# Node-ordered accumulator columns and one contiguous one-hot per edge tile in a two-layer graph network kernel

## The reference, cut to what matters

```python
h = relu(layernorm(x))                                    # stage 0
# two layers (layer 0, layer 1): norm = dis[src] * dis[dst], with a self loop for every node
h = h @ W
h = segment_sum(h[src] * norm[:, None], dst) + b
h = layernorm(tanh(h)) * g + be
x = x + h                                                 # after layer 1
h = relu(layernorm(x))                                    # layer 2 (edge features)
aggr = segment_sum(relu(h[src] + edge_attr), dst)
h = relu((h + aggr) @ W1 + b1) @ W2 + b2
out = x + relu(h)
```

## Time and profile before

| | |
|---|---|
| median of 3 runs | 2889.8 us (2885.09 to 2891.92) |
| the profiled execution | 2884.79 us, of which the span of the profile is 2883.0 us |
| mean granted TensorE clock | 0.899 |
| busy share of the span | PE 73%, PEld 65%, DVE 81%, ACT 70%, POOL 62% |
| DMA | 523.50 MB in all, mean 182 GB/s |

### The profile page before, as it was taken

How to read it: one execution, slowest core, us unless ns; L and a number is a source line. 1 busy time by engine, 2 the same in 40 slices (tenths; PEclk the granted TensorE clock), 3 DMA queues, 4 the chain that set the end, 5 groups by cost and what they waited for, 6 DMA issues and landing times.

```text
span 2883.0 us, 53972 instructions
## 1 busy us (share of the span) xinstructions
PE 2100.9 (73%) x15433; PEld 1879.5 (65%) x15433; DVE 2332.1 (81%) x8137; ACT 2016.7 (70%) x5708; POOL 1785.3 (62%) x2717
## 2 busy tenths in 40 slices
PE   0200028999999886577777777788289999999988
PEld 0100028888889876467667676677168888887877
DVE  4999848888889784499999799899868787777665
ACT  0039966888888594476666566667488999988766
POOL 4025667777777726787676765664377776765540
PEclk9999999999999887778888788878589999999879
DMA  0059957888888665245544455444356665655443
GB/s 14 1 216 383 370 199 239 280 278 279 277 286 283 206 241 168 78 148 157 157 150 145 144 158 157 125 150 138 123 143 179 181 177 171 173 166 158 142 116 104
DMA packets 262164, 523.50 MB, mean 182 GB/s; under 512 B 101225, under 2 KB 102260, under 8 KB 261864
## 3 DMA queue, kind: packets, MB, share of 16 engines
q1 hardware_dynamic: 217325, 451.15, 45.9%
q0 software_dynamic: 43680, 68.58, 11.0%
q10 hardware_dynamic: 859, 0.23, 0.0%
HBM read 324.98 MB, written 194.81 MB: 180 GB/s over the span
## 4 chain that ended last, share of the span: by engine, by line
PE 37%; DVE 28%; POOL 13%; ACT 12%; issue 6%; DMA 3%; SPq 1%; POOLq 0%; ACTq 0%; DVEq 0%
PE ps L1263 17%; POOL got_f_ L702 12%; DVE hot_ L938 7%; ACT rows_f_ L1079 6%; PE ps L1298 6%; PE ps L1308 5%; PE ps L1248 4%; DVE stat_b_ L873 4%; PE ps L1279 3%; DVE stat_a_ L873 3%; DMA got_f_<-table,src_of 3%; DVE hot_p_ L767 2%; DVE y_f_ L1002 2%; DVE low_f_ L912 2%; ACT rows_f_ L1116 1%
## 5 line engine op out<-in xcount | busy, mean ns | idle before, releaser
L702 POOL DMA_INDIRECT got_f_<-table,src_of x1365 | 1448.7, 1061 | 703.7 <-issue 369.4
L1263 PE MATMUL ps<-hot_,high_f_ 128*96 128x304 f32 (+46 forms) x3750 | 1020.7, 309 | 303.5 <-DVE hot_ L938 300.7
L1263 PE MATMUL ps<-hot_,low_f_ 128*96 128x304 f32 (+46 forms) x3750 | 991.2, 303 | 0.0
L1263 PEld LDWEIGHTS ps<-hot_,high_f_ 128*96 128x96 f32 (+1 forms) x3750 | 684.0, 182 | 381.7 <-issue 215.7
L938 DVE TENSOR_SCALAR hot_<-node_at,dst_of 128x368 fp32r<-128x368 f32 (+33 forms) x1875 | 837.7, 486 | 37.8 <-PE ps L1263 36.1
L1263 PEld LDWEIGHTS ps<-hot_,low_f_ 128*96 128x96 f32 (+1 forms) x3750 | 687.1, 183 | 32.4 <-issue 0.2
L1104 ACT ACTIVATE y_f_<-ps,ds 128x96 f32<-128x96 f32 x1568 | 386.5, 372 | 247.8 <-POOL rows_f_ L689 174.0
L1092 ACT COPY z_f_<-ps 97x1024 f32<-97x1024 f32 (+2 forms) x294 | 300.5, 1022 | 193.7 <-PE ps L1263 192.9
L1248 PE MATMUL ps<-ident_f,in_f_ 128*97 128x128 f32 (+1 forms) x1568 | 223.3, 290 | 265.5 <-DMA in_f_<-table 265.5
L873 DVE BATCH_NORM_STATS2 stat_a_<-y_f_ 128x6 f32<-128x96 f32 x1952 | 383.9, 242 | 2.9 <-ACT y_f_ L1104 2.9
L1248 PEld LDWEIGHTS ps<-ident_f,in_f_ 128*97 128x97 f32 (+1 forms) x1568 | 195.8, 179 | 265.8 <-DMA in_f_<-table 265.8
(11 more groups left out here) (117 smaller groups left out, 2816.3 us busy)
## 6 DMA issues: line engine op xcount, KB each, us to landing
x_f_<-in_x SPq DMA_DIRECT2D x146, 384.0 KB, 5.4
table<-rows_f_ SPq DMA_DIRECT2D x98, 396.0 KB
in_f_<-table SPq DMA_DIRECT2D x98, 396.0 KB
table<-rows_f_ SPq DMA_DIRECT2D x98, 392.0 KB
in_f_<-table SPq DMA_DIRECT2D x98, 392.0 KB
table<-rows_f_ SPq DMA_DIRECT2D x98, 388.0 KB
in_f_<-table SPq DMA_DIRECT2D x98, 388.0 KB
skip<-x_f_ SPq DMA_DIRECT2D x97, 384.0 KB, 3.5
```

The lines of the kernel that those rows point to most:

```text
L702: pool.indirect_dma_start(out=got_f[g][:, u * w:(u + 1) * w], out_offset=None, in_=table[:, :], in_offset=bass.IndirectOffsetOnAxis(ap=src ...
L1263: last = pe.matmul(acc[0:w, h, :].rearrange("m (s p) -> m s p", p=P)[:, :, p0:p0 + pw], part[:, u * wide_w:u * wide_w + w], hot_view(slot, ...
```

## The change

The partition order of a block is altered to two half blocks: slab group h (4 of the 8 slabs) holds nodes of half block h, and partition p holds nodes `512h + 4p` to `512h + 4p + 3` of it. With this, an accumulator column can be the node's own number in its block: column `c` of bank `h` is node `512h + c`. A transpose of slab s then writes columns `s % 4, s % 4 + 4, ...` (a step of four), one-hots are contiguous ranges of nodes, and `evict` reads the accumulator with a step of four and writes slabs in a row, so that `z_f` is as before. A one-hot is now made once for each tile (a tile whose band crosses into another block keeps its one-hot for the second block), and a pair has only the pieces (bank, first column, width, offset in the one-hot) that its band touches: two matmuls for each piece. Bands are rounded to 2 nodes and not to 16. Every plain transfer of a block moves 256 runs of half the length (1536 bytes for 96-wide rows) in place of 128. Transfers of the short last block to and from x and the output are two. The core of the diff:

```diff
-                lo = max(first, int(lo) // (2 * slabs) * 2 * slabs)
-                hi = min(stop, -(-math.ceil(hi) // (2 * slabs)) * 2 * slabs)
+                lo = max(first, int(lo) // 2 * 2)
+                hi = min(stop, -(-math.ceil(hi) // 2) * 2)
...
-                    for b in range(lo // block, -(-hi // block)):
-                        p0, p1 = (max(lo, b * block) - b * block) // slabs, (min(hi, (b + 1) * block) - b * block) // slabs
-                        use.append((place[b], q, u, b, p0, p1 - p0))
+                    cuts = [lo, hi] if hi - lo <= block else [lo, *range((lo // block + 1) * block, hi, block), hi]
+                    for lo, hi in zip(cuts, cuts[1:]):
+                        k = len(self.tiles)
+                        self.tiles.append((q, u, lo, hi))
+                        use += self.uses(place, block, k, lo, hi)
...
+    def uses(self, place, block, k, lo, hi):
+
+        found = []
+        for b in range(lo // block, -(-hi // block)):
+            pieces = []
+            for h in range(2):
+                bank = b * block + h * block // 2
+                c0, c1 = max(lo, bank), min(hi, bank + block // 2)
+                if c0 < c1:
+                    pieces.append((h, c0 - bank, c1 - c0, c0 - lo))
+            found.append((place[b], k, pieces))
+        return found
...
+        def move(eng, i, table, tile, done, load, whole=True):
+
+            lo = plan.at[i] * BLOCK
+            if whole or lo + BLOCK <= N:
+                far = table[ds(lo, BLOCK), :].rearrange("(h p q) d -> p h (q d)", h=2, q=S // 2)
+                near = tile[:, :, :].rearrange("p (h q) d -> p h (q d)", h=2)
+                eng.dma_start(near if load else far, far if load else near).then_inc(done, 16)
+                return
...
-                for m in plan.pairs_at[i]:
-                    q, u, b, p0, pw = plan.pairs[m]
-                    slot, turn = hot_slot(layer, m)
+                for k in plan.tiles_at[i]:
+                    q, u, lo, hi = plan.tiles[k]
+                    slot, turn = hot_slot(layer, k)
...
                     if turn >= HOTS:
-                        dve.wait_ge(pair_done, turn - HOTS + 1)
+                        b_layer, b_k = divmod(turn - HOTS, TILES)
+                        dve.wait_ge(pair_done, b_layer * PAIRS + plan.last_of[b_k] + 1)
                     c = plan.quads[q][1] + u
-                    dve.tensor_scalar(hot_view(slot, pw), node_at[:, :, 0:pw], float(b * BLOCK + p0 * S),
-                                      dst_of[:, c:c + 1], ALU.add, ALU.is_equal).then_inc(hot_ready_f, 1)
+                    dve.tensor_scalar(hot[slot][:, 0:hi - lo], node_at[:, 0:hi - lo], float(lo), dst_of[:, c:c + 1],
+                                      ALU.add, ALU.is_equal).then_inc(hot_ready_f, 1)
...
-                act.copy(z_f[i % 2][0:w, :].rearrange("p (h c) -> p h c", h=2), ps[done % 2][0:w, :, :]
-                         ).then_inc(evicted, 1)
+                act.copy(z_f[i % 2][0:w, :].rearrange("m (h q p) -> m h q p", h=2, q=S // 2),
+                         ps[done % 2][0:w, :, :].rearrange("m h (p q) -> m h q p", q=S // 2)).then_inc(evicted, 1)
...
-                    k = s % 4 * P
-                    last = pe.matmul(acc[0:w, s // 4, k:k + P], own[:, s, 0:w], ident_f[:, :], start=s % 4 == 0,
+                    to = acc[0:w, s // 4, :].rearrange("m (p q) -> m q p", q=S // 2)[:, s % 4, :]
+                    last = pe.matmul(to, own[:, s, 0:w], ident_f[:, :], start=s % 4 == 0,
...
-                    for h in range(2):
+                    for h, c0, n, a in pieces:
                         for part in (high_f[f], low_f[f]):
-                            last = pe.matmul(acc[0:w, h, :].rearrange("m (s p) -> m s p", p=P)[:, :, p0:p0 + pw],
-                                             part[:, u * wide_w:u * wide_w + w],
-                                             hot_view(slot, pw)[:, h * S // 2:(h + 1) * S // 2, :],
-                                             start=False, stop=m == plan.pairs_at[i][-1] and part is low_f[f],
-                                             skip_group_check=True)
+                            last = pe.matmul(acc[0:w, h, c0:c0 + n], part[:, u * wide_w:u * wide_w + w],
+                                             hot[slot][:, a:a + n], start=False,
+                                             stop=m == plan.pairs_at[i][-1] and part is low_f[f], skip_group_check=True)
```

More of the change, by code:

```diff
@@ L130, in __init__ @@
         self.first_place = [place[b] for b, _ in supers]
-        self.quads, self.pairs, self.pairs_at, use = [], [], [[] for _ in range(blocks)], []
+        self.quads, self.tiles, self.pairs, self.pairs_at, use = [], [], [], [[] for _ in range(blocks)], []
         for i in self.order:
@@ L140, in __init__ @@
                     lo, hi = self.bands[self.slot_of[i] + t + u]
[L141 to L146 removed]
+                    cuts = [lo, hi] if hi - lo <= block else [lo, *range((lo // block + 1) * block, hi, block), hi]
[3 more added lines that the diff above has]
+                        use += self.uses(place, block, k, lo, hi)
+        self.last_pair, self.first_use, self.last_use = [0] * len(self.quads), [blocks] * len(self.quads), [0] * len(self.quads)
+        self.first_of, self.last_of = {}, {}
+        self.tiles_at = [[] for _ in range(blocks)]
+        for m, (pos, k, pieces) in enumerate(sorted(use)):
+            q = self.tiles[k][0]
+            self.pairs.append((k, pieces))
             self.pairs_at[pos].append(m)
+            if k not in self.first_of:
+                self.first_of[k] = m
+                self.tiles_at[pos].append(k)
+            self.last_of[k] = m
             self.last_pair[q] = m
@@ L209, in gnn_kernel @@
     TILES_MAX = CHUNK
+    TILES = len(plan.tiles)
+    assert all(plan.last_of[k - HOTS] < plan.first_of[k] for k in range(HOTS, TILES))
+    assert max(hi - lo for _, _, lo, hi in plan.tiles) <= BLOCK
     assert GROUPS4 == 4 and SUPERS <= 128 and all(plan.pairs_at) and plan.at.index(BLOCKS - 1) >= X_RING + Y_RING
@@ L508, in table_written, with moved, hot_slot @@
                 eng.wait_ge(stored[j], stored_before(stage + 1, j))
[L510 to L515, removed]
+        def move(eng, i, table, tile, done, load, whole=True):
[5 more added lines that the diff above has]
+                return
+            for h in range(2):
+                rows_n = min(HB, N - lo - h * HB)
+                parts = rows_n // (S // 2)
+                far = table[ds(lo + h * HB, rows_n), :].rearrange("(p q) d -> p (q d)", q=S // 2)
+                near = tile[0:parts, h * (S // 2):(h + 1) * (S // 2), :].rearrange("p q d -> p (q d)")
+                eng.dma_start(near if load else far, far if load else near).then_inc(done, 16)
+        def moved(i, ring):
+            turns = range(i % ring, i + 1, ring)
+            return 16 * (len(turns) + (plan.at.index(BLOCKS - 1) in turns))
+        def hot_slot(layer, k):
+            n = layer * TILES + k
             return n % HOTS, n
@@ L643, in fast_sync @@
                     sp.wait_ge(out_done, k + 1)
-                    parts = parts_at(k)
-                    sp.dma_start(rows(out, plan.at[k], parts),
-                                 y_f[k % Y_RING][0:parts, :, :].rearrange("p s d -> p (s d)")
-                                 ).then_inc(out_stored[k % Y_RING], 16)
+                    move(sp, k, out, y_f[k % Y_RING], out_stored[k % Y_RING], False, whole=False)
             for j in range(Y_RING):
-                sp.wait_ge(out_stored[j], 16 * len(range(j, BLOCKS, Y_RING)))
+                sp.wait_ge(out_stored[j], moved(BLOCKS - 1 - (BLOCKS - 1 - j) % Y_RING, Y_RING))
         def prologue_pool(pool):
@@ L684, in add_x @@
                     k = i % X_RING
-                    pool.wait_ge(x_in_f[k], 16 * (len(range(k, BLOCKS, X_RING)) + i // X_RING + 1))
+                    last = k + (BLOCKS - 1 - k) // X_RING * X_RING
+                    pool.wait_ge(x_in_f[k], moved(last, X_RING) + 16 * (i // X_RING + 1))
                     if i % 4 == 0 and stored_before(2, i // 4):
@@ L976, in shift_x @@
                 k = i % X_RING
[L977 removed]
+                dve.wait_ge(x_in_f[k], moved(i, X_RING))
                 if i < X_RING:
@@ L1255, in gather_edges @@
                 for m in plan.pairs_at[i]:
-                    q, u, _, p0, pw = plan.pairs[m]
-                    slot, turn = hot_slot(layer, m)
+                    k, pieces = plan.pairs[m]
+                    q, u, _, _ = plan.tiles[k]
+                    slot, turn = hot_slot(layer, k)
                     f, quad_turn = high_slot(layer, q)
```

40 lines of the change are left out of this document (14 added, 26 removed).

## The result

The changed kernel takes 3047.9 us (median of 4 runs, 3038.5 to 3056.1) against 2887.5 us (2884.3 to 2891.9) for the kernel before on the same chip: ratio 1.0553 (95% interval 1.0518 to 1.0588). It is slower by 160 us; forecast were 51 us less. The profiled execution has a span of 3036.0 us at a mean granted clock of 0.875.

The account below looks back on a forecast made before the run. Bounds: ACT in stage 0, POOL's gathers in layer 0, DVE in most of layer 1, PE in layer 2. Gains of 2, 19 and 30 us sum to 51: 2889.8 - 51 = 2839 us, range 2808 to 2896.

Parts of the forecast that it names:

- One-hots: Making one-hots on DVE: 625 to 548 in a layer, 19 us less DVE work each; the ring's new wait costs nothing.
- that lead: Ring of one-hots: six tiles reach further than six pairs, and a block's first one-hot often exists already; wait costed at nothing.
- Its last sign of being wrong: Layer 1, where four engines wait on each other, moving by more than 30 us either way would show the prediction wrong.
- Layer 2: PE bounds it; 33 us less matmul work, less the block 87 rest and a little lost to ACT: 30 us gained.
- Block 87: Slow-clock block: PE's 27.65 us of matmuls would become 17, but DVE comes next at 22; 5.5 us taken.
- Layer 0: POOL's 455 gathers set the pace and do not change; only emptying the line after the last gather gains 2 us.
- Layer 1: DVE bounds most of it: 16 us from 19 us less one-hot work, plus 3 from block 87, 19 us gained.
- Rival B: PE pays for the step: transposes doubled, 1.04 us more a block, sum about +60, 2950 us; chance 0.09.
- Rival A: ACT pays for the step in the eviction, 7.6 us a block in layer 2: 2879 us, up to 2900; chance 0.14.
- Rival C: Layer 1: earlier one-hots and less PE work shorten the ring of waits by another 25 us, 2814 us; chance 0.13.
- Rival D: Layers 0 and 1 give savings back through less granted clock; smaller transfers cost stage 0 18 us: 2878 us; chance 0.09.
- The lead of 42 us: Stage 0: x is loaded 20 blocks ahead, 42 us, which covers up to 18 us of dearer half-length transfers.

Follow-up runs that it names:

- the ring in order: The renumbered kernel, but PE waits for the count that the old number by tile asked for, where higher: 2917.4 us, 1.0082 to the kernel before.
- the ring out of order: The changed kernel, numbers left as they are for the ring, but PE waits for the count at which its tile is made: 2840.6 us, 0.9833.
- the renumbered kernel: The changed kernel with tiles numbered in the order in which DVE makes their one-hots, ring and waits as they were: 2832.3 us, 0.9806.
- the longer ring: The changed kernel with one tile of 6144 one-hot columns given out by width in place of six buffers of 1024: 2921.8 us, 1.0129.
- a first experiment: The changed kernel with a one-hot for each (tile, block) pair again, 625 in a layer, same ring of six: 3229.8 us, 1.1212.

## Why the prediction was wrong, point by point

**The step that failed** is in "One-hots": "The ring of six now holds tiles, not pairs. The new wait, for a tile used in two blocks, can make DVE stand behind that tile's second block ... I cost it at nothing; the cover is that lead." It looked at one side, DVE's wait for a buffer, and took for granted that PE's wait for a one-hot still meant the one-hot that PE needs. Before, pairs were numbered in the order in which both engines went through them, and number and count were one; after, the number is the tile's, the order is still the block's, and they part where a band wider than a block is cut. The kernel's text shows it: `pe.wait_ge(hot_ready_f, turn + 1)` stayed as it was, while `turn` now came from the list of tiles, and DVE's loop over `tiles_at`. Printing the order of making against the numbers, an arithmetic like the one done for the matmuls, would have found 56 of 548 out of place. What it costs (85 us with the ring in order, 216 with it out of order) no row of before could have told; that it isn't nothing, the prediction's own sentence could have told: moments and row work stand between the one-hots of a block and those of the next. Its last sign of being wrong, layer 1 moving by more than 30 us, came true with 100. As the cover of the ring's wait, the lead held: alone, the ring out of order costs 8 us and a ring of four 13.

**The rest of the sum held**, in total, and that in part by luck: the renumbered kernel is what the prediction took the change to be, and has 2832 us, 55 less than before, where 2839 and 51 less were forecast. But layers 0 and 1 missed by 13 us each, one up and one down. By layer (first load to first load, profiled executions; layer 2 to the end):

| | before | after | renumbered | forecast gain | gain, renumbered |
|---|---|---|---|---|---|
| layer 0 | 690 | 729 | 674.8 | 2 | 15 |
| layer 1 | 996.5 | 1096.6 | 990.1 | 19 | 6 |
| layer 2 | 796.5 | 809 | 765.4 | 30 | 31 |

*Layer 2* came out by its own step: matmuls 1794 in place of 2500, and PE still the bound. Windows of the renumbered kernel, layer 0, layer 1, layer 2:

```profile
402.00:1030.00 628.00, 558.25 (x3964) 498.06 (x3965) 516.62 (x1915) 491.68 (x1639) 483.27 (x455) 0.93 0.86 271
...
1077.00:2067.00 990.00, 679.77 (x4146) 589.67 (x4146) 852.34 (x3240) 611.51 (x1792) 653.03 (x553) 0.79 0.48 143
...
2071.00:2832.00 761.00, 721.76 (x4538) 571.62 (x4538) 563.58 (x1122) 657.97 (x1533) 474.70 (x452) 0.96 0.58 162
```

PE is busy 721.8 of 761 us: 34.5 less than the 756.2 of the earlier trace rows, the stretch 32 shorter. Block 87 gave more of it than the 5.5 us forecast, since DVE did not set its pace at 22 us. Its matmuls in the renumbered kernel begin at 2726.92, and `hide` behind them at 2744.45, 17.5 us later where it was 27.5; that is the 17 us that PE's own price gave. So the other blocks gave some 21 us of the 31.

```profile
2726.92 0.29 PE L1300 MATMUL ps<-hot_,high_f_ 128*96 128x4 f32 x1 [10.13 <-DVE hot_ L974]
...
2744.45 1.94 PE L1333 MATMUL ps<-z_f_,mw1s_f 96*96 96x512 f32 x4
```

*Layer 0* gained 15, not 2, since a term stood there as fixed that is not. POOL still sets the pace, with issue gaps as most of its idle time, but the 455 gathers of the layer took 483.3 us against 496.0 in the kernel before, 13 of the 15 us. That this is the change's doing is not shown. The gathers of layer 0 in the kernel before, in that kernel with half-length runs, in the renumbered kernel, and in the renumbered kernel with one-hots by pair:

```profile
L702 POOL DMA_INDIRECT got_f_<-table,src_of x455 | 496.0, 1090 | 147.3 <-issue 125.9 <-PE ps L1263 12.5 <-DMA table<-rows_f_ 8.9
```

```profile
L714 POOL DMA_INDIRECT got_f_<-table,src_of x455 | 489.7, 1076 | 147.6 <-issue 128.0 <-PE ps L1275 10.4 <-DMA table<-rows_f_ 9.2
```

```profile
L737 POOL DMA_INDIRECT got_f_<-table,src_of x455 | 483.3, 1062 | 147.3 <-issue 125.0 <-PE ps L1300 13.4 <-DMA table<-rows_f_ 8.9
```

```profile
L737 POOL DMA_INDIRECT got_f_<-table,src_of x455 | 496.4, 1091 | 147.6 <-issue 124.6 <-PE ps L1300 13.7 <-DMA table<-rows_f_ 9.3
```

The layer took 690, 683.7, 674.8 and 688.0 us in them: it goes with its gathers, and these differ by 6 us without the change and by 13 with it. The median gather takes 947 ns before and renumbered, so it is the long ones (up to 3.7 us before, 2.9 renumbered) that got fewer or shorter; why, the runs don't tell.

*Layer 1* gained 6, not 19. DVE's work fell by 18 us, from 870.4 to 852.3, the 19 of the forecast nearly. The waits of that layer in the renumbered kernel:

```profile
PE ps L1300 <- DVE hot_ L974: 247.0, 97, 30.3
ACT y_f_ L1140 <- POOL rows_f_ L724: 189.1, 25, 32.9
...
DVE stat_b_ L908 <- POOL rows_f_ L724: 89.7, 9, 30.5
```

PE's wait for DVE rose by 19 us against the earlier trace rows: what PE and DVE saved, they stand for others. ACT and DVE wait up to 33 us at a time for POOL's row work. The step "DVE busy 87% of the time: 16" was too high, since a share of busy time says nothing of whether DVE ends the stretch last. Which link sets this layer is open; no run was made for it.

**Rival B (PE pays for the step)** ended on the right side by a wrong mechanism. The kernel was slower, as B says, but the transposes did not spread. Eight of them in layer 2 of the renumbered kernel, and all 784 of that layer in the kernel after (ns min/median/max):

```profile
2244.11 1.04 PE L1284 MATMUL ps<-ident_f,x_f_ 128*96 128x128 f32 x8
```

```profile
L1278 PE MATMUL ps<-ident_f,x_f_ x784: 269/273/450, 2243.0 to 3014.9; 128*96 128x128 f32 x196
```

1.04 us for eight with a step of 16 bytes, as in the earlier trace rows without one. The sentence of the Trainium skill ("Advanced Engine Details and Errata", PSUM Cachelines) that any non-contiguous pattern significantly slows matmuls down did not hold for these transposes. Nor is it borne out by the matmuls of edges: in the kernel before they wrote a bank in four separate runs of columns, one for each slab (480 columns as four of 120), and their starts stood 0.22 us apart, 0.46 ns a column; in the kernel after they write one contiguous run, and 366 columns stand 0.16 us apart (595.78 and 595.94 above), 0.44 ns. The prediction had overlooked these four runs as the nearest row for a broken pattern. What a step of four columns would do to those faster matmuls, no run here shows.

**Rival A (ACT pays)** is refuted as well. The eviction in the kernel after:

```profile
L1122 ACT COPY z_f_<-ps x294: 984/1012/1106, 419.1 to 3018.4; 97x1024 f32<-97x1024 f32 x49, 99x1024 f32<-99x1024 f32 x49, 96x1024 f32<-96x1024 f32 x49
```

A median of 1012 ns for 1024 columns with a step; the same line of the kernel before has a median of 1012 contiguous (its mean in layer 2 was 1.00 us). The price of the earlier trace rows, 1.1 ns an element for DVE's step of 24 bytes in SBUF, does not carry over to ACT reading PSUM with 16. The rival's sum did not follow from its own terms either: ACT at 7.6 us a block would stay under the 756 us that PE had before, so layer 2 would not have grown by 10 us.

**Rival C** (layer 1 gains 25 more) is refuted; that layer gained less. **Rival D** was half right in what it says of layer 1, where most of a saving off the bound was given back, but in waits and not by the clock: in the renumbered kernel PE is busy 680 us there against 712, at 0.79 against 0.80. It was wrong on stage 0: that took 229 us for 228. There the cover was thinner than forecast: over 232 to 352 us the DMA share reads 1.06 where it was 1.00, and a block of x takes 9.9 us to land, where it took 5.1 in the same stretch before. The lead of 42 us held, and ACT still works without a gap. A window of the kernel after:

```profile
232.00:352.00 120.00, 0.00 (x0) 0.00 (x0) 106.80 (x735) 120.00 (x341) 73.29 (x174) 1.00 1.06 376
```

The transfers of 200 to 380 us, before and after (count, size, median us to landing):

```profile
x_f_<-in_x SPq DMA_DIRECT2D x35, 384.0 KB, 5.1
...
x_f_<-in_x SPq DMA_DIRECT2D x36, 384.0 KB, 9.9
```

**The range**, 2808 to 2896, priced unknown costs of hardware at some length and gave a wait in the kernel's own arithmetic none. No case for "the new order of waits is not what it says" was among the rivals, though a wait had been re-keyed from pairs to tiles.

## What to carry to other kernels

A semaphore that counts what a producer has made tells "item n is ready" only if n is its place in the producer's program. When a change gives items new numbers, write the producer's order out beside the numbers, for each engine that waits by them; a number too high is no race and no wrong result, only a wait for something later. (A number too low would be a race, if no earlier wait covered it; here one did.) The sign in the profile was a pair of waits that face each other, though with the longer ring only one of the two was left; the sure sign is, in order of time, a consumer that starts just after the item *behind* its own; and a first experiment that makes a suspected cost smaller and the kernel slower is the best lead of all.

## What the runs showed of the hardware

- Fp32 transposes that write PSUM with a step of 16 bytes, and ScalarE reads of 1024 PSUM columns with it, take the time of contiguous ones: medians of 273 against 272 ns, and 1012 in both.
- Matmuls of edges that write a PSUM bank in four runs of columns keep the pace of contiguous ones: 0.46 and 0.44 ns a column.
- Runs of 1536 bytes in place of 3072 cost 4.6% of the queue's time and nothing of the kernel's (ratio 0.9998, 0.9983 to 1.0013); where the DMA share was already 1.00, the kernel before so altered had a block of x landing in 9.8 us in place of 5.1.
- The 455 gathers of layer 0, the same work in every kernel, took 483 to 496 us in the profiled executions.
- A ring shortened from six to four made DVE wait 142 us more and the kernel 13 us longer: most of an engine's wait can lie beside other work.
